# Attention and experts on one core: where the expert weights of the last batch are split, when Silu's table is loaded, when the projection begins

## The reference

```
q = layernorm(x) @ Wq;  k, v = split(ctx @ Wkv)
x = x + concat_heads(softmax(q k^T / 8) v) @ Wproj + bproj
h = layernorm(x)
p = top2(softmax(h @ gate_w)), divided by their sum
x = x + sum over the two of p * ((silu(h @ gate[e]) * (h @ up[e])) @ down[e])
```

## Time and profile before

| | |
|---|---|
| median of 3 runs | 1570.44 us (1569.52 to 1571.47) |
| the profiled execution | 1568.5 us, its span 1566.4 us |
| TensorE busy | 1503.0 us, 96% of the span |
| VectorE, ScalarE, GpSimd busy | 968.7, 762.3, 555.2 us |
| TensorE's mean granted clock | 0.986 of full |

### The profile page before, as it was taken

The page is one execution under the profiler, slowest core; times in us unless marked ns, Lnnn a source line. Parts: engine busy times, 40 slices in busy tenths (PEclk is TensorE's granted clock), DMA queues, the critical chain, the costliest instruction groups (busy, mean ns, idle before and its releaser), DMA issues. The chain is left out here.

```text
span 1566.4 us, 37570 instructions
## 1 busy us (share of the span) xinstructions
PE 1503.0 (96%) x12134; PEld 1321.0 (84%) x12135; DVE 968.7 (62%) x2579; ACT 762.3 (49%) x2091; POOL 555.2 (35%) x636
## 2 busy tenths in 40 slices
PE   4999999999999999999999999999996699999997
PEld 4888888898888888888888888898875588888886
DVE  5667677676766676767767676667675633333332
ACT  3555555555555555555555555555553322222221
POOL 5224233333433243423334343324355122323232
PEclk9999999999999999999999999999997799999999
DMA  5411111111112221111111111221016233332332
GB/s 152 131 50 50 56 49 55 49 55 50 54 54 60 64 73 54 49 54 49 54 49 57 49 54 54 65 69 52 12 66 227 52 52 51 50 54 47 53 50 28
DMA packets 82704, 96.19 MB, mean 61 GB/s; under 512 B 6912, under 2 KB 77808, under 8 KB 82672
## 3 DMA queue, kind: packets, MB, share of 16 engines
q1 hardware_dynamic: 68960, 74.67, 16.5%
q0 software_dynamic: 12144, 15.66, 6.2%
q10 hardware_dynamic: 1568, 5.44, 1.0%
HBM read 44.85 MB, written 50.90 MB: 61 GB/s over the span
## 5 line engine op out<-in xcount | busy, mean ns | idle before, releaser
L767 ACT ACTIVATE prob<-bank,neg_max 112x375 f32<-112x375 f32 x512 | 295.3, 586 | 138.1 <-DVE neg_max L1017 138.1
L1017 DVE TENSOR_REDUCE neg_max<-bank 112x1 f32<-112x375 f32 x512 | 243.9, 539 | 19.4 <-PE bank L1247 19.3
L1257 PE MATMUL bank<-ident,prob 112*125 112x112 f32 x1536 | 214.7, 274 | 2.6 <-ACT prob L767 2.4
L1257 PEld LDWEIGHTS bank<-ident,prob 112*125 112x125 f32 x1536 | 195.9, 188 | 13.8 <-ACT prob L767 4.9
L706 POOL DMA_INDIRECT out<-y_out,dest_now x63 | 97.8, 1552 | 244.1 <-ACT y_out L859 215.0
L895 DVE TENSOR_TENSOR K_l<-bank,K_h 128x376 fp32r<-128x376 f32 x256 | 140.4, 550 | 64.9 <-ACT K_h L727 62.4
L1281 PE MATMUL bank<-probT,V 125*64 125x112 f32 x3072 | 176.6, 264 | 2.0 <-DVE probT L1023 1.1
L1155 PE MATMUL bank<-Wgu,hT_h 128*128 x504 | 175.1, 429 | 2.9 <-DVE hT_l L1112 2.9
L1281 PEld LDWEIGHTS bank<-probT,V 125*64 125x64 f32 x3072 | 149.1, 137 | 14.6 <-issue 2.6
L885 DVE COPY V<-bank 125x512 f32<-125x512 f32 x96 | 66.4, 692 | 151.3 <-PE bank L1219 147.4
L1133 DVE COPY hidT<-bank 128x512 f32<-128x512 f32 x63 | 43.6, 692 | 173.7 <-PE bank L1462 173.7
(11 more groups left out here) (171 smaller groups left out, 3719.9 us busy)
## 6 DMA issues: line engine op xcount, KB each, us to landing
bins<-pad_rows SPq DMA_DIRECT2D x29, 1032.0 KB, 6.2
h_in<-bins SPq DMA_DIRECT2D x63, 129.0 KB, 2.2
y_sb<-in_ctx SPq DMA_DIRECT2D x32, 187.5 KB, 2.4
y_sb<-in_ctx SPq DMA_DIRECT2D x62, 93.8 KB, 2.5
Wgu<-in_L_ffn_gate_up_w SPq DMA_DIRECT2D x4, 1024.0 KB, 5.2
Wgu<-in_L_ffn_gate_up_w ACTq DMA_DIRECT2D x4, 1024.0 KB, 13.2
x_sb<-in_x SPq DMA_DIRECT2D x16, 224.0 KB, 2.8
x_res<-in_x SPq DMA_DIRECT2D x32, 112.0 KB, 5.6
```

The costliest lines, as they stand in the source:

```text
L767: nc.scalar.activation(prob[:, j, :], S_ps[j][0:LQ, 0:LKV], ACT.Exp, bias=neg_max[:, j:j + 1], accum_out=row_sum[:, head // HB, head % HB: ...
L1017: nc.vector.tensor_reduce(neg_max[:, j:j + 1], S_ps[j][0:LQ, 0:LKV], AX.X, ALU.max, negate=True).then_inc(max_done, 1)
L1257: last = nc.tensor.transpose(S_ps[j][0:KR, t * LQ:t * LQ + LQ], prob[:, j, t * KR:t * KR + KR], ident[0:LQ, 0:LQ])
```

## The change

Six edits. GpSimd: expert 2 is split right after expert 1, ahead of the normalised rows of batch 30 (before: behind them, the output split and a scatter). ScalarE: the high part of expert 3 is made in step 1 of batch 31 (before: in i = 16, behind the loads of 6 and 7); 4 to 6 there, 7 ahead of the plan (before: 3 and 4 there, 5 ahead of the plan, 6 and 7 behind the first rows' high part). ScalarE: one Silu of a column is run before the plan, into a new tile `table`. VectorE: the low part of expert 3 is made at the end of step 3 of batch 31 (before: in i = 16). TensorE, in every batch: `project` waits for the first eight heads' low part, runs 12 products, waits for the second, runs the other 12, in the same order of sums.

```diff
@@ GpSimd, pair(i)
                     if known(i) and i == NP - 1 and odd:
                         split_expert(1)
+                        split_expert(2)
...
-                    if known(i) and i == NP - 1 and odd:
-                        split_expert(2)
@@ ScalarE, pair(i) and behind it
+                        if known(i) and i == NP - 1 and odd and s == 1:
+                            hi_of_experts(3, 4)
...
-                            hi_of_experts(3, 5)
+                            hi_of_experts(4, 7)
...
-            hi_of_experts(5, 6)
+            hi_of_experts(7, E)
+            nc.scalar.activation(table[:], ident[:, 0:1], ACT.Silu)
...
             hi_of_rows(0, 0)
-
-            hi_of_experts(6, E)
@@ VectorE, pair(i)
-                        if known(i) and i == NP and not odd and s == 1:
+                        if known(i) and i == NP - 1 and odd and s == 3:
                             lo_of_expert(3)
@@ TensorE, project(b)
-                pe.wait_ge(OT_lo, 2 * b + 2)
                 if known(b) and b == 0:
                     pe.wait_ge(wp_done, 2)
-                split_product(C_ps[0:LQ, 0:C], [(OT_h[:, j, :], OT_l[:, j, :], WpH[:, j, :], WpL[:, j, :])
-                                                for j in range(NJ)]).then_inc(proj_made, 1)
+                for half in range(2):
+                    pe.wait_ge(OT_lo, 2 * b + half + 1)
+                    for j in range(HALF * half, HALF * half + HALF):
+                        for n, (w, m) in enumerate(((OT_h, WpH), (OT_h, WpL), (OT_l, WpH))):
+                            last = mm(C_ps[0:LQ, 0:C], w[:, j, :], m[:, j, :], start=j == 0 and n == 0,
+                                      stop=j == NJ - 1 and n == 2)
+                last.then_inc(proj_made, 1)
```

More of the change, by code:

```diff
@@ L293, in attention_and_experts @@
         inv_top = sb("inv_top", [LQ, 1], F32)
+        table = sb("table", [P, 1], F32)
         wd_at = base + size - E * FJ * C * 4
```

## The result

The changed kernel takes 1575.16 us (median of 9 runs, 1573.62 to 1575.46) against 1570.39 us (9 runs, 1568.29 to 1571.47) of the kernel before: ratio 1.0029, 95% interval 1.0019 to 1.004, so it is slower, by some 4.6 us. The forecast was 1573.5 us; the measured time stands at the upper edge of the 1571.8 to 1575.2 that the prediction gave to its own path. The profiled execution took 1575.45 us (span 1573.3).

The account below looks back on a forecast made before the run. Bound: the last batch's end of attention, where TensorE idles, up to the first expert tiles. x +3.5, gates +0.5, casts -0.95 sum to +3.1 us on the median of 1570.44: 1573.5 us; range 1571.0 to 1577.0, own path 1571.8 to 1575.2.

Parts of the forecast that it names:

- its own path: The main forecast for the last batch: ScalarE stalls, clock falls and returns; 1573.5 us, range 1571.8 to 1575.2, chance 0.50.
- Stall: ScalarE, batch 31: cast of expert 3 waits for its load; first exponential of step 2 at 1193.83 instead of 1181.49.
- Clock: TensorE, batch 31: half clock after 9.8 us without work, back during the scores; O_now 11.2 us late.
- O_now to x: End of attention, batch 31: output split and projection take 4.45 us instead of 12.15; x 3.5 us late.
- Gates behind the cast of expert 6: ScalarE, batch 31: gates wait for that cast in the queue; costs 0.5 us, bounds 0 and 1.5.
- Casts and table load: Before tile 1: VectorE's 0.95 us wait for a cast goes, bounds 0.9 and 1.3; table load's 1.28 brings nothing more.
- Contention on GpSimd's side: VectorE's bookkeeping of batch 29 slowed beside GpSimd's split until 1182.9; x of batch 30 some 0.45 late, bounds 0 and 2.
- The rival with more contention: GpSimd's split holds VectorE more: 2 us on x of batch 30 and so on the load; 1575 us, chance 0.09.
- The second wait: TensorE's projection in all other batches: wait met beforehand, cost taken as 0; upper bound 30 times 0.02.
- The rival without a stall: Cast of expert 3 doesn't hold ScalarE; gates 2.8 us early, with 0.95 for the casts: 1566.7 us, chance 0.06.

Follow-up runs that it names:

- e3: The kernel before with only ScalarE's cast of expert 3 moved up to step 1: 1582.22 us, ratio 1.0077.
- e5: The changed kernel with SyncE's load of expert 3, and the down weights behind it, ahead of its wait for x of batch 30: 1564.12 us, ratio 0.9963.
- e2: The kernel before with only GpSimd's split of expert 2 moved up: 1568.36 us, ratio 0.998.
- e1: The kernel before with only the projection in two parts, with its second wait: 1568.41 us, ratio 0.9982.
- e11: e8 with the projection in one piece behind one wait, as in the kernel before: 1562.87 us, ratio 0.9961.
- e9: e8 without the Silu of one column ahead of the plan: 1560.06 us, ratio 0.9942.
- e4: The changed kernel with ScalarE's cast and VectorE's subtraction of expert 3 back in their old places: 1569.69 us, ratio 0.9992.
- e7: e4 with ScalarE's casts of experts 5 and 6 behind the gates of batch 31: 1563.46 us, ratio 0.996.
- e6: e5 with ScalarE's casts of experts 5 and 6 behind the gates of batch 31: 1562.72 us, ratio 0.9952.
- e8: e6 with GpSimd's split of expert 2 waiting for VectorE's bookkeeping of batch 29: 1560.42 us, ratio 0.9938.

## Why the prediction was right

The path went as the steps said; each against its own bound.
- **Stall.** First exponential 42.07 from the zero against 30.36: 11.7 us late, 12.3 forecast. Transposes 9.2 late (42.79 against 33.61), 9.8 forecast. The load left 0.10 us later (34.75 against 34.65) instead of 0.45. e3 and e5 show the cause from both sides: the cast alone makes the loss, the load moved ahead of SyncE's wait removes it.
- **Clock.** Half for transposes and products, back within the scores, as taken: scores 10.75 late (11.0 forecast), O_now 11.06 late (11.2 forecast).
- **O_now to x.** 4.36 us (4.45 forecast), x 3.27 late (3.5 forecast). Alone, the split moved ahead gives 4.2 (e2) and the second wait 1.7 (e1); without the second wait 2.8 of the 7.8 us are missing (e11).
- **Gates behind the cast of expert 6.** The term that was mis-sized: 0.5 forecast, bounds 0 and 1.5; it is 1.84 (gates 5.11 late, x 3.27), outside the bounds. Three things make the missing 1.3, within 0.1. My own numbers gave 0.8 (cast done at 1217.6, gates wanted at 1216.8), and I took 0.5. x came 0.2 earlier than forecast. And the cast of expert 6 ended 0.9 later (1221.2 against 1217.6, with the trace 2.70 later): I let the four loads land one behind the other at 2.6 us. From their casts: expert 4 landed at 1212.40, 5.0 us after its issue, 5 at 1216.37, 4.0 later, 6 near 1219.3, 7 some 2.4 after that. 6 and 7 were issued while 5 was on its way; that they shared its bandwidth fits this, but no run tests it. The path of the trace adds up to 3.27 + 1.84 - 1.05 = 4.1 us, 1.0 over my sum; these two traces end 4.2 apart, and the rest to the 4.6 of the ratio stays open.
- **Casts and table load.** 1.05 back where 0.95 was forecast, and e9 confirms that the table load adds nothing.
- **Contention on GpSimd's side.** VectorE's bookkeeping ended at 1185.40, as forecast (1182.9, with the trace 2.70 later: 1185.6). x of batch 30 came 0.11 later from the zero than before (33.92 against 33.81). That this is so little is luck of the two traces: the last product of projection 30 began 1.1 us earlier here (32.40 against 33.49). Before, x came 0.32 us after that last product began; here it came 1.52 after, as it waited for VectorE. In the six kernels with the split at this place (changed, e2, e4 to e7) x of batch 30 stands at 33.92 to 33.98, whether the last product of projection 30 began at 30.9 or at 32.5. And the load of expert 3 follows that x. In e3, the same stall without the split, that product began at 32.50, the load left at 33.66 instead of 34.75 and the exponentials began at 41.36 instead of 42.07. So the stall did not hide the contention; some 0.7 us of it are in the changed kernel's exponentials, and with the stall gone it was 1.6 us at O_now (e6 against e8). The rival with more contention, at 1575, has the measured time but not by its mechanism: it wanted x of batch 30 2 us late.
  The Trainium skill (GPSIMD Engine Reference, Specifications) names contention of GpSimd with VectorE instructions in a two-port mode or with two SBUF inputs. `chosen` has two such inputs; top_f has one, and no trace here shows its mode. By that rule the split should not lie beside such instructions, and e8 agrees, with 0.17 us for 4.42.
- **The second wait.** Nothing in the loop, as forecast (e1).

The rival without a stall was priced at 1566.7 us; e5, which is that case, took 1564.12. Its gates came 4.25 us earlier than before, where the rival had 2.8: it let them wait for the cast of expert 6 until 1210.5 (59.4 from the zero), and in e5 they start at 57.93.

## What to carry to other kernels

When work on a loaded buffer is moved ahead on one engine, look at where its load is issued: an in-order queue on another engine can hold it behind a wait that has nothing to do with it, and everything behind the moved work pays. What is on the path should stand ahead of work that only has to be done in time, also where both look short: here the gates behind a cast cost 1.8 to 3.0 us. Three edits of one change, each run alone, ranged from 12 us lost to 3 us won; that found the one whose partner edit was missing. e8, at 0.9938 (0.9925 to 0.9952) of the kernel before, is the change with that partner, the gates ahead of the casts of 5 and 6, and GpSimd's split behind VectorE's bookkeeping.

## What the runs showed of the hardware

A VectorE instruction on 112x8 elements with two SBUF inputs lasted 4.42 to 4.45 us when it began just after a GpSimd subtraction of 128x2048 had begun; it ended when that had ended, in the six kernels with the split at that place (changed, e2, e4 to e7); `onehot`, also with two inputs, had begun 0.02 us ahead of the subtraction in the changed kernel (1180.58, 1180.60) and took 0.17 us. GpSimd's own cast took 2.08 us instead of 1.89 beside VectorE's. The Silu followed its table load of 1.28 us at once where its input was there (1229.40 and 1230.69 in the trace of before). Four loads of 1 MB from one queue, issued in two pairs 2.1 us apart, did not land at even distances in the changed kernel's trace: 4.0 us between the first and the second, 2.9 and 2.4 between the others, as their casts show.
